# Attention heads and an ODE guess on one core: the values group spread over three turns, the first distances among the projections, the guess with its weights moving

## The reference, cut to what matters

```python
def _L2_attn_ref(x, W_qkv, rel_table, W_out, b_out):      # after a layer norm, result added to x
    q, k, v = jnp.split(x @ W_qkv, 3, axis=-1)            # 8 heads of 16
    dots = jnp.einsum('bhid,bhjd->bhij', q, k) * SCALE
    dist = jnp.clip(seq[:, None] - seq[None, :], -128, 128) + 128
    dots = dots + jnp.einsum('bhnd,nrd->bhnr', q, rel_table[dist]) * SCALE
    attn = jax.nn.softmax(dots, axis=-1)
    out = jnp.einsum('bhij,bhjd->bhid', attn, v)
    return out.transpose(0, 2, 1, 3).reshape(b, n, 128) @ W_out + b_out

def _L2_ffn_ref(x, W1, b1, W2, b2, W3, b3):               # 1023 steps from the first token
    f(y) = tanh(tanh(y @ W1.T + b1) @ W2.T + b2) @ W3.T + b3      # 128 -> 512 -> 512 -> 128
    y <- y + dt * (k1 + 2 * k2 + 2 * k3 + k4) / 6
```

## Time and profile before

| | us |
|---|---|
| median of 3 runs (lowest, highest) | 1853.8 (1850.9, 1855.29) |
| profiled execution, its own time | 1859.48 |
| its span | 1857.5 |
| PE, DVE, ACT, POOL busy | 1565.8, 918.1, 875.8, 293.7 |
| mean granted TensorE clock | 0.903 |

### The profile page before, as it was taken

One profiled execution on the slowest core, in us unless ns is written; L12 is line 12 of the kernel. 1 busy time (PEld: TensorE's weight loads), 2 busy tenths in 40 slices (PEclk: granted clock), 3 DMA queues, 4 the chain that ended last, 5 costly groups with the idle time before them and its releaser, 6 DMA issues. The chain is left out here.

```text
span 1857.5 us, 29879 instructions
## 1 busy us (share of the span) xinstructions
PE 1565.8 (84%) x12240; PEld 813.6 (44%) x12240; DVE 918.1 (49%) x1425; ACT 875.8 (47%) x1195; POOL 293.7 (16%) x122
## 2 busy tenths in 40 slices
PE   3689999989777977999999996888999999639588
PEld 1222222222334745666666665773444444216254
DVE  5658888888733535677666772000011100258242
ACT  1647777777433344677777763222223222140521
POOL 0036666666210000000000000000000000020000
PEclk7879999999898986999999997558999999869889
DMA  1000000000010004343344420000000000000000
GB/s 61 0 1 2 2 2 2 2 2 2 1 72 14 1 1 159 128 157 146 138 148 159 159 80 1 0 0 0 1 0 0 0 0 0 28 1 3 1 1 23
DMA packets 20654, 69.63 MB, mean 37 GB/s; under 512 B 688, under 2 KB 17072, under 8 KB 18096
## 3 DMA queue, kind: packets, MB, share of 16 engines
q1 hardware_dynamic: 20240, 66.79, 9.7%
q10 hardware_dynamic: 288, 1.05, 0.2%
HBM read 33.24 MB, written 34.60 MB: 37 GB/s over the span
## 5 line engine op out<-in xcount | busy, mean ns | idle before, releaser
L482 POOL TENSOR_TENSOR l_work<-l_a_scores,l_work 128x2048 f32<-128x2048 f32 x64 | 232.8, 3640 | 219.3 <-PE banks L599 117.3
L1725 PE MATMUL banks<-s_h,pack_l2f_l3f 128*128 128x512 f32 x512 | 221.0, 592 | 0.0
L1752 ACT ACTIVATE s_h<-banks,pack_l2f_l3f 128x512 f32<-128x512 f32 x128 | 87.9, 687 | 250.6 <-PE banks L1725 175.8
L540 DVE TENSOR_TENSOR l_work<-banks,sc_negc 128x1024 f32<-128x1024 f32 x128 | 156.4, 1222 | 49.8 <-PE banks L646 33.5
L599 PE MATMUL banks<-l_work,pack_l 32*32 32x512 f32 x4096 | 160.3, 607 | 22.8 <-ACT l_work L502 19.5
L502 ACT ACTIVATE l_work<-banks,pack_l 128x1024 f32<-128x1024 f32 x128 | 142.6, 1114 | 77.5 <-PE banks L599 76.7
L1350 PE MATMUL banks<-pack_l2a,r_e 128*128 128x128 f32 x1024 | 144.4, 284 | 39.3 <-ACT r_e L1403 39.3
L1442 DVE TENSOR_REDUCE r_raw<-banks 128x1 f32<-128x640 f32 (+1 forms) x128 | 109.5, 856 | 111.7 <-PE banks L1331 111.7
L1403 ACT ACTIVATE r_e<-banks,r_max 128x1024 f32<-128x1024 f32 x128 | 142.4, 1113 | 41.3 <-DVE r_max L1448 39.7
L1331 PE MATMUL banks<-r_k,r_q 32*128 32x128 f32 (+3 forms) x832 | 151.0, 471 | 0.6 <-DVE r_rd L1473 0.6
L1725 PEld LDWEIGHTS banks<-s_h,pack_l2f_l3f 128*128 128x128 f32 x512 | 97.3, 190 | 122.5 <-issue 122.5
(11 more groups left out here) (357 smaller groups left out, 2219.2 us busy)
## 6 DMA issues: line engine op xcount, KB each, us to landing
distances<-r_rd SPq DMA_DIRECT2D x16, 2048.0 KB, 6.9
r_band<-distances SPq DMA_DIRECT2D x16, 1536.0 KB, 7.0
pack_l2f_l3f<-pack_dram_l2f SPq DMA_DIRECT2D x1, 2148.5 KB, 10.6
pack_l2f_l3f<-pack_dram_l3f SPq DMA_DIRECT2D x1, 1248.5 KB, 5.8
pack_l<-pack_dram_l SPq DMA_DIRECT2D x1, 1217.0 KB, 6.7
residual<-x ACTq DMA_DIRECT2D x2, 512.0 KB, 7.9
out<-residual SPq DMA_DIRECT2D x2, 512.0 KB, 3.1
pack_l2a<-pack_dram_l2a SPq DMA_DIRECT2D x1, 715.0 KB, 4.5
```

What stands on the lines that cost most here:

```text
L482: pool.tensor_tensor(image(H1R[:, c % 3]), bc(a, 2, 16), bc(b, 3, HW), ALU.add).then_inc(sem("added"), 1)
L540: dve.tensor_tensor(image(H2M[:, (2 * c + part) % 3]), image(PS[:, MAX + j:MAX + j + 2]), bc(NEGC[:, j:j + 2, n, i, rows(half)], 3, HW), A ...
L1725: ins = pe.matmul(bank, W["w2"][:, col:col + P], H1[:, c, m], start=(m == 0), stop=(m == HB - 1))
```

## The change

1. The projections move into the heads' block, so the barrier between them goes. Their groups now stand in the list `PROJECTED`: 4 queries of image 0, 8 first distances of image 0, 4 queries and 8 distances of image 1, then keys and values. At the first distance of an image PE waits until all groups before are evicted. POOL fills the ends of the first two pairs too.
2. `values` is cut in two parts of 4 matmuls, and both parts and `pick` stand between scores and transposes: in turn s PE does scores(s), the first part of s-2, the second of s-3, pick of s-4, back(s-1). ACT's `group_out` and DVE's `outputs` come one turn later.
3. In the guess the loop is unrolled. W2 is the moving operand (256 columns, two halves) and the activations, 128x64, are the weights; b2 comes in by two matmuls of 32 rows by 256 columns; the integration matrix is applied ahead of W3; the result is Y0 plus b3 times the node's time, added by DVE. In the last round the hidden layer is transposed instead. The spreading over the steps is shared by ACT and DVE.

```diff
+PROJECTED = ("q", "q", "q", "q") + ("d",) * 8 + ("q", "q", "q", "q") + ("d",) * 8 + ("k", "x") * 4 + ("v",) * 4
...
+            elif kind == "d":
+                b, t = divmod(n, ITILES)
+                a = n % 2
+                r = 64 * a
+                if t == 0:
+                    pe.wait_ge(sem("act_out"), done(g - 1, True))
+                    pe.wait_ge(sem("dve_out"), done(g - 1, False))
+                pe.matmul(bank[:, 0:REL], Qm[r:r + 32, a, 0, b * PIX + t * P:b * PIX + (t + 1) * P], W["rel"][r:r + 32],
+                          start=True, stop=True, tile_position=(r, 0)).then_inc(sem("made"), 1)
...
-        def values(s):
+        def values(s, part):
             i, b, t = place(s)
-            if s // GT:
-                pe.wait_ge(sem("o_out"), s // GT)
-            pe.wait_ge(sem("pt_act"), s + 1)
-            pe.wait_ge(sem("pt_dve"), s + 1)
+            if part:
+                pe.wait_ge(sem("pt_dve"), s + 1)
+            else:
+                if s // GT:
+                    pe.wait_ge(sem("o_out"), s // GT)
+                pe.wait_ge(sem("pt_act"), s + 1)
...
-        for s in range(ALL + 3):
+        for s in range(ALL + 4):
             if s < ALL:
                 scores(s)
+            if last(s - 2):
+                values(s - 2, 0)
+            if last(s - 3):
+                values(s - 3, 1)
+            if last(s - 4):
+                pick(s - 4)
             if 0 <= s - 1 < ALL:
                 back(s - 1)
-            if last(s - 2):
-                values(s - 2)
-            if last(s - 3):
-                pick(s - 3)
...
-        for s in range(ALL + 4):
-            if last(s - 3):
-                group_out(s - 3)
+        for s in range(ALL + 5):
+            if last(s - 4):
+                group_out(s - 4)
...
+                for h in range(2):
+                    pe.matmul(PS[0:N, 1 + h, 0:HALF_H], W["to_nodes"][N:N + 32], W["to_steps"][N:N + 32, h * HALF_H:(h + 1) * HALF_H],
+                              start=True, stop=False, tile_position=(N, 0))
+                for h in range(2):
                     for m in range(HB):
-                        c = (m * HB + k) * P
-                        ins = pe.matmul(PS[:, 1, k * N:(k + 1) * N], W["w2"][:, c:c + P], H1[:, m], start=(m == 0),
+                        if h == 0:
+                            pe.wait_ge(sem("h1"), g * HB + m + 1)
+                        c = m * HB * P + h * HALF_H
+                        ins = pe.matmul(PS[0:N, 1 + h, 0:HALF_H], H1[:, m], W["w2"][:, c:c + HALF_H], start=False,
                                         stop=(m == HB - 1))
```

More of the change, by code:

```diff
@@ L1178, in l2_project @@
     ends = (W["rel"][:, 0:1], W["rel"][:, REL - 1:REL])
-    on_act = lambda g: (g - g // 2 % 2 if BANKS <= g < KGROUPS else g) % 2 == 0
     flat = lambda v: v.rearrange("p s k -> p (s k)")
[L1181 to L1199, removed]
+    index = lambda g: PROJECTED[:g].count(PROJECTED[g])
@@ L1200, in _ @@
                 for k, at in enumerate(extra(a, b)):
-                    ins = pe.matmul(bank[:, k * P:(k + 1) * P], w, XN[:, at:at + P], start=True, stop=True)
+                    ins = pe.matmul(bank[:, k * P:(k + 1) * P], W["wk"][:, a * P:(a + 1) * P], XN[:, at:at + P],
+                                    start=True, stop=True)
                 ins.then_inc(sem("made"), 1)
-            for g in range(KGROUPS, VGROUPS):
-                bank = group(g)
+            else:
                 for j in range(4):
-                    t = 4 * (g - KGROUPS) + j
+                    t = 4 * n + j
@@ L1207, in _ @@
                     ins = pe.matmul(bank[:, j * P:(j + 1) * P], XN[:, t * P:(t + 1) * P], W["wv"], start=True, stop=True)
                 ins.then_inc(sem("made"), 1)
[L1210 to L1244, removed]
@@ L1481, in _ @@
                 top(s)
-            if last(s - 4):
-                outputs(s - 4)
+            if last(s - 5):
+                outputs(s - 5)
     @block.gpsimd
     def _(pool):
-        for f in range(NB, HB_ALL):
-            pool.wait_ge(sem("rd"), (f - NB + 1) * ITILES)
+        for f in range(HB_ALL):
+            if f < NB:
+                g = 12 * f + 11
+                pool.wait_ge(sem("act_out"), sum(ON_ACT[k] for k in range(g + 1)))
+                pool.wait_ge(sem("dve_out"), sum(not ON_ACT[k] for k in range(g + 1)))
+            else:
+                pool.wait_ge(sem("rd"), (f - NB + 1) * ITILES)
             ends(pool, f % NB, "ends")
@@ L1609, in _ @@
+            for n in range(0, NCH, 2):
                 dve.wait_ge(sem("steps"), n + 1)
[L1610 removed]
+                dve.tensor_scalar(Y[:, n * CH:(n + 1) * CH], PS[:, STEPS[n]], Y0[:, n // 2:n // 2 + 1], None, ALU.add)
         @block.scalar
         def _(act):
[L1614 removed]
+            for g in range(GUESSES):
                 for k in range(HB):
[L1616 to L1617 removed]
+                    act.wait_ge(sem("z1"), g * HB + k + 1)
+                    act.activation(H1[:, k], PS[:, FIRST[k], 0:N], ACT.Tanh, bias=W["b1"][:, k:k + 1]
@@ L1638, in _ @@
[L1638 to L1644 removed]
+                    ins.then_inc(sem("z2"), 1)
@@ new lines, in _ @@
+                last = g == GUESSES - 1
+                for h in range(2):
+                    pe.wait_ge(sem("h2"), 2 * g + h + 1)
+                    for m in (2 * h, 2 * h + 1):
+                        out, hidden = PS[:, 3 + h, m % 2 * N:m % 2 * N + N], H2[:, m * P:(m + 1) * P]
+                        if last:
+                            ins = pe.transpose(out, hidden, W["ident"])
+                        else:
+                            ins = pe.matmul(out, hidden, W["to_nodes"][0:N], start=True, stop=True)
+                    ins.then_inc(sem("g"), 1)
@@ new lines, in _ @@
+                for m in range(HB):
+                    pe.wait_ge(sem("g_out"), 2 * g + m // 2 + 1)
+                    w3 = W["w3"][:, m * P:(m + 1) * P]
+                    if last:
+                        ins = pe.matmul(PS[0:N, MOVED, 0:P], G[:, m], w3, start=(m == 0), stop=(m == HB - 1))
+                    else:
+                        ins = pe.matmul(PS[:, MOVED, 0:N], w3, G[:, m], start=(m == 0), stop=(m == HB - 1))
+                ins.then_inc(sem("moved"), 1)
+            pe.wait_ge(sem("f"), 1)
```

234 lines of the change are left out of this document (139 added, 95 removed).

## The result

The changed kernel takes 1884.1 us (median of 4 runs, 1881.6 to 1886.5), the one before in the same comparison 1854.6 (1850.9 to 1858.4). The ratio is 1.0159, with a 95% interval of 1.0134 to 1.0184: **1.6% slower**, 29.5 us. The profiled execution took 1881.56 with a span of 1879.8, against 1859.48 and 1857.5: 22 us more.

The account below looks back on a forecast made before the run. It took the guess as a half-clock chain bound longest by weight loads, the heads as nearly PE-bound. Terms -10.8 - 7 + 2 + 67 - 45 - 3 = +3.2 on 1859.5 gave 1862.7, less 5.7: 1857 us, range 1782 to 1888.

Parts of the forecast that it names:

- Turn 0 earlier: Start of the heads: turn 0 gets its minimum at about 718 instead of 728.9, -10.8 us (bounds -5 and -12).
- Turns at full clock: First five turns of the heads: clock at 1.00, about 2.45 us each instead of 3.85, -7 us.
- Groups at full clock: Groups of the heads: 12.24 us against 12.23, with pick waiting 0.8 for `og`; +2 us over 31 groups.
- Falls: Heads: thin stretch around pick drops the clock in every second group, 15 times at 4.5 us each, +67 us.
- The guess: Guess rounds: clock rises in the first round, one or two later falls, -45 us; spreading at the end, -3 us.
- the clock holds: Rival, heads: no falls, the 67 us vanish, 1790 us; faster with fewer than 14 falls; chance 0.16.
- Pick finds `og` ready: Rival, heads: ACT reaches `group_out` ahead of the exponential, no wait or thin stretch, 1765 us; chance 0.04.
- The guess stays at 1.2 GHz: Rival, guess: clock stays low, gain 2 to 3 us instead of 48, total 1903 us; chance 0.10.

Follow-up runs that it names:

- `a_fill32`: Changed kernel with four matmuls of 128 columns on 32 rows, output never read, added ahead of each pick; 1814.8 us.
- `p_bridge`: Changed kernel with pick behind the transposes and unread dense matmuls in PE's waits outside the groups (first exponential, output layer, norm, nodes); 1771.8 us.
- `a_oldorder`: Changed kernel with the heads' old order put back (values whole and pick, both behind the transposes); new projections and guess stay; 1807.5 us.
- `a_fill`: Changed kernel with four matmuls of 128 columns on 128 rows, output never read, added ahead of each pick; 1811.8 us.
- `a_ogearly`: Changed kernel with ScalarE's group copy moved ahead of the exponential of the turn before, pick still ahead of the transposes; 1790.6 us.
- `a_fill17`: Changed kernel with four matmuls of 17 columns on 128 rows, output never read, added ahead of each pick; 1864.0 us.
- `b_project`: Kernel before with the new projections alone (first distances amid them, end fills on GpSimd, no barrier), heads' order and guess as before; 1843.9 us.

## Why the prediction came out as it did

The profiled executions differ by 22.1 us; I had +3.2. Term by term:

- **Turn 0 earlier, -10.8.** The first band operation is at 717.55 instead of 728.90, 11.35 earlier, of which 1.8 come from a phase that began earlier (688.89 against 690.66). What is left is -9.6. It no longer waits for the transfer; what holds turn 0 now is PE, which reaches it at 715.18.
- **Turns at full clock, -7.** Half right. PE waits 1.72 us for the first exponential, and the clock falls even so, but for two turns instead of five:

```profile
715.18 0.70 PE L1343 MATMUL banks<-r_k,r_q 32*128 32x256 f32 x2 [1.12 <-DVE r_v L1287]
...
717.55 0.49 DVE L1455 CUSTOM_DVE_ANT_0 banks<-banks,r_band,r_raw 128x256 f32<-128x256 f32 x1 [0.15 <-DVE r_raw L1449]
...
719.30 1.71 PE L1362 MATMUL banks<-pack_l2a,r_e 128*128 128x128 f32 x8 [1.72 <-ACT r_e L1414]
```

  Three turns at 1.4 less are about -4. I had not walked turn 0 itself, only its neighbours.
- **Groups at full clock, +2.** Right: 12.25 for 12.24, and the mechanism with it (the copy behind the exponential, a wait of 0.68 for 0.8).
- **Falls, +67.** The mechanism was right, the size nearly: 18 falls of 4.1 us, 74, where I had 15 of 4.5. That every second group would have one was a guess that no row supported; that it came so near (17 of 31) was luck. My reason for them was only partly right. I held 32-row matmuls to be as good as nothing; `a_fill32` shows that they hold the clock nearly as well as full ones.
- **The guess, -45 and -3.** It gave 39.2 (1203.35 to 1287.63 against 1142.22 to 1265.67). High rounds are 8.19 for 7.7, the first 11.89 for 11.7, and instead of one or two falls there are four:

```profile
1203.35 1.97 PE L1652 MATMUL banks<-g_y,pack_l2f_l3f 128*128 128x64 f32 x8 [2.13 <-DVE g_y L1614]
...
1215.24 1.10 PE L1652 MATMUL banks<-g_y,pack_l2f_l3f 128*128 128x64 f32 x8 [0.32 <-DVE g_y L1625]
...
1223.43 1.10 PE L1652 MATMUL banks<-g_y,pack_l2f_l3f 128*128 128x64 f32 x8 [0.32 <-DVE g_y L1625]
...
1226.09 6.38 PE L1662 MATMUL banks<-pack_l2f_l3f,g_h 128*64 128x256 f32 x16
```

  Two of the falls cost a round 1.7 us, the other two 3.3 each (11.51 for 8.19, and the last round 11.24 for 7.91 in `p_bridge`). I had taken 0.96 for W1 and 3.45 for W2; they take 1.03 and 3.60, and the four matmuls of either later layer 1.1 each.

The misses are 9 us of the guess, 7 of the falls, 3 of the first turns and 1 of the band, less the 1.8 from the earlier phase: 18 of the 19. The other 8 us of the 27 are not in the kernel. I took 5.7 us off because the profiled execution of before stood above its median; the profiled one of after stands 2.5 below its own.

Of the rivals, "the clock holds" needed 14 falls or fewer to come out faster; there were 18, though the kernels that keep the clock up, `a_oldorder`, `a_fill` and `a_fill32`, show what it would have been worth: 1807 to 1815 where I had put 1790, short by about the same guess and median. "Pick finds `og` ready" did not happen by itself; made to happen in `a_ogearly` it gives 1790.6, where I had put 1765. "The guess stays at 1.2 GHz" did not come either: with W2 on 64 columns of the array the clock rose at 1211.1, in the first round.

The net is a change with three good parts and one call in the wrong place: 46 us gained by the projections and the guess, 71 lost by the order, of which the spreading of values is innocent.

## What to carry to other kernels

Before moving small matmuls (few columns, loads of weights) to where PE waits, look at what then stands in a row between two dense stretches; a wait of 0.7 us, worth 22 us in all by itself (32 groups of 0.68), cost 74 by the clock. The page's share of busy time will not warn of it: after such a move read the granted clock in windows, and where it fell, what PE did just ahead. Dense matmuls that nobody reads, put into a wait, are a cheap test of whether a stage suffers from the wait or from the clock, and where the wait can't be removed they can be the cure as well.

## What the runs showed of the hardware that was not expected

- A PE that was busy 15.80 of 16.00 us fell to 1.2 GHz, with 17-column matmuls in the mix (`a_fill17`, 11 such falls in the groups); with 128-column matmuls in the same place and as busy it never fell (`a_fill`). With 128 columns on 32 rows it fell twice in 395 us, and never behind a stretch in which it had waited (`a_fill32`).
- Alike stretches do not all bring a fall: 17 of 31 did in the changed kernel.
- Once low, busy PE did not bring the clock back at once: 11.09 us busy of 11.09 at 0.54, and the old guess stayed at 0.50 for all its 115.62 us, yet runs at 1.00 throughout when it is entered dense and its waits are filled.
- The same code in the first turns was low for 7 us in one program (`b_project`) and for 17 in another (`a_oldorder`).
